# An AdaLN-FFN kernel on one core: the two low-rank sessions of each step made one, with the down products and the outputs moved behind it

## The reference

```python
# block 0: gated FFN with a low-rank adapter for each sequence, then a layer with a binarised weight
gate = x @ W_gate.T + 0.5 * (x @ A_gate[i].T) @ B_gate[i].T      # 512 -> 1376, rank 16
up   = x @ W_up.T   + 0.5 * (x @ A_up[i].T)   @ B_up[i].T
act  = silu(gate) * up
down = act @ W_down.T + 0.5 * (act @ A_down[i].T) @ B_down[i].T  # 1376 -> 512
x1 = x + down @ sign(weight).T + bias0
# block 1: rank-16 adapter for each sequence, then a layer with 8 summed adapters
z  = (x1 @ B1[k].T) @ A1[k].T
out = x1 + z @ W1.T + bias1 + 2 * sum_n w_n * (z @ lora_A[n].T) @ lora_B[n].T
```

## Time and profile before

| | us |
|---|---|
| median of 3 runs (862.29 to 863.07) | 863.04 |
| the profiled execution | 861.99 |
| its span | 860.2 |
| PE busy | 851.8 |
| DVE busy | 636.8 |
| ACT busy | 290.1 |
| POOL busy | 83.4 |

### The profile page before, as it was taken

The page is one execution under the profiler, slowest core; times in us unless marked ns, Lnnn a source line. Parts: engine busy times, 40 slices in busy tenths (PEclk is TensorE's granted clock), DMA queues, the critical chain, the costliest instruction groups (busy, mean ns, idle before and its releaser), DMA issues.

```text
span 860.2 us, 22295 instructions
## 1 busy us (share of the span) xinstructions
PE 851.8 (99%) x7384; PEld 695.8 (81%) x7384; DVE 636.8 (74%) x1362; ACT 290.1 (34%) x535; POOL 83.4 (10%) x122
## 2 busy tenths in 40 slices
PE   8999999999999999999999999999999999999998
PEld 5887788878888888888888888888888788888885
DVE  5697787868777786867778686777878686777764
ACT  4862333323233332323233332333333232323310
POOL 0202100101010010101001010100001010100101
PEclk9999999999999999999999999999999999999999
DMA  9969987869789796979889796978979797987953
GB/s 341 415 246 339 322 266 230 275 214 303 249 282 279 247 280 211 279 241 311 253 255 294 217 278 220 312 242 291 269 243 261 227 298 238 294 268 243 288 142 109
DMA packets 171356, 227.31 MB, mean 264 GB/s; under 512 B 59200, under 2 KB 128832, under 8 KB 163648
## 3 DMA queue, kind: packets, MB, share of 16 engines
q1 hardware_dynamic: 108480, 106.57, 42.2%
q10 hardware_dynamic: 60416, 111.27, 37.6%
q0 software_dynamic: 2432, 9.11, 2.7%
HBM read 178.69 MB, written 16.97 MB: 227 GB/s over the span
## 4 chain that ended last, share of the span: by engine, by line
PE 94%; DMA 2%; DVE 2%; ACTq 0%; POOL 0%; ACT 0%; issue 0%; SPq 0%; DVEq 0%
PE gu_ps L1246 52%; PE y_ps L1367 27%; PE gu_ps L1476 3%; PE out_ps L1389 3%; PE out_ps L1440 2%; PE y_ps L1246 1%; PE gu_ps L1467 1%; PE out_ps L1376 1%; PE out_ps L1246 1%; DMA t_table<-t_lo 1%; DMA x_in<-in_x 1%; PE out_ps L1397 1%; DVE vt_raw L987 0%; PE gu_ps L1367 0%; DMA lb_raw<-in_lbw 0%; POOL vt_table L602 0%
## 5 line engine op out<-in xcount | busy, mean ns | idle before, releaser
L1367 PE MATMUL y_ps<-down_sb,actT_sb 128*128 128x512 f32 x1023 | 248.1, 395 | 0.0
L1367 PEld LDWEIGHTS y_ps<-down_sb,actT_sb 128*128 128x128 f32 x1023 | 189.6, 188 | 59.6 <-issue 21.4
L626 ACT CAST actT_sb<-landed 128x512 fp32r<-128x512 f32 (+1 forms) x96 | 51.5, 582 | 130.7 <-issue 107.2
L578 POOL TENSOR_TENSOR b_two<-b_raw,const_sb 128x128 f32<-128x128 f32 x62 | 26.7, 451 | 656.7 <-DMA b_raw<-in_b1tab 656.7
L1246 PE MATMUL gu_ps<-wg_sb,xT_sb 128*128 128x432 f32 x384 | 82.3, 363 | 0.5 <-DVE act_all L915 0.5
L1246 PE MATMUL gu_ps<-wu_sb,xT_sb 128*128 128x432 f32 x384 | 81.7, 361 | 0.0
L1246 PEld LDWEIGHTS gu_ps<-wg_sb,xT_sb 128*128 128x128 f32 x384 | 71.0, 188 | 5.7 <-DVE xT_sb L897 1.4
L1246 PEld LDWEIGHTS gu_ps<-wu_sb,xT_sb 128*128 128x128 f32 x384 | 70.9, 188 | 4.2
L897 DVE TENSOR_TENSOR vslot<-vslot_raw,vslot 128x864 fp32r<-128x864 f32 x61 | 62.5, 1065 | 11.3 <-ACT vslot L626 11.2
L1246 PE MATMUL gu_ps<-slot,s_sb 128*128 128x512 f32 x270 | 69.0, 390 | 0.0
L919 DVE STREAM_TRANSPOSE act_all<-act_all 128x512 f32<-128x512 f32 (+1 forms) x96 | 64.1, 667 | 3.3
(11 more groups left out here) (188 smaller groups left out, 1263.7 us busy)
## 6 DMA issues: line engine op xcount, KB each, us to landing
slot<-t_table ACTq DMA_DIRECT2D x59, 1024.0 KB, 8.7
vslot_raw<-vt_table ACTq DMA_DIRECT2D x60, 432.0 KB, 4.1
a_raw<-in_atab SPq DMA_DIRECT2D x128, 152.0 KB, 7.6
rows_sb<-in_btab SPq DMA_DIRECT2D x128, 118.0 KB
landed<-act_all SPq DMA_DIRECT2D x190, 64.0 KB, 4.2
x_in<-in_x SPq DMA_DIRECT2D x31, 256.0 KB, 2.7
out_x<-out_sb SPq DMA_DIRECT2D x31, 256.0 KB, 5.2
xT_raw<-in_xT ACTq DMA_DIRECT2D x30, 256.0 KB, 3.3
```

The source lines that it names most:

```text
L578: nc.gpsimd.tensor_tensor(b1_two[:, n].rearrange("p k e r -> p e k r"), rows, ones, ALU.mult).then_inc(L["b1_moved"], 1)
L626: return nc.scalar.copy(o, i)
L1367: last = nc.tensor.matmul(to[:], actT_sb[:, ACTT_SLOT[c] + n, a, :], down_sb[:, blk, b, :], start=begin and (c, n) == (0, 0) and (a, b) == ...
```

## The change

One session a step. The small products now stand directly ahead of the row products, and are those of the **next** step for t (g + 1), of the step before for td (g - 1) and of three steps before for t1 (g - 3). They go into spare columns (from 432 on) of the SIDE and FIRST banks of `gu_ps`, which DVE sets to zero ahead of them (`clear`, three a step; PE waits for `cleared` before it writes these banks). The row products use td of g - 2 and t1 of g - 4. All 33 down products of g - 2 run at the start of step g, and y is complete when the row products have added their part. Each engine's step is split into `step` (ahead of the session) and `behind` (after it); DVE's `turn_t` for the next step, `split_xT`, `own_t1`, `own_td`, `turn_x1` and `add_out` stand in `behind`. x1 is made in place of x in `x_in`; POOL adds the bias from there into `x1_two[parity]`, a pair of buffers, where `add_out` adds in place and from where SP stores. The transposed x1 has places of its own over buffers that are idle then. The A-down rows have a buffer (`ad_raw`) and DMAs of their own, issued by ACT; loads of xT, slots and side blocks are issued earlier in ACT's step. The first six steps are written out instead of four. `finish` of each engine works off the longer pipeline: SP issues the sbd, and three sets of c rows, for the end (`c_end`) there.

The diff, cut to its core (removed functions are in the listing above):

```diff
...
-        x1_turn = x_in
+        x1_two = [place(f"x1_{n}", [P, H], f32) for n in range(2)]
...
+        t_at, td_at, t1_at = (gu_ps[5], SIDE), (gu_ps[3], SIDE), (gu_ps[2], SIDE)
...
+        def load_ad(engine, at):
+            for b in range(GB):
+                engine.dma_start(ad_raw[:, b, :], atab[bass.ds(at[b], P), AW:AW + ADW]).then_inc(L["ad_in"], 16)
...
+            def store(g, parity, signal=L["stored"]):
...
+                sp.dma_start(out[bass.ds(g * P, P), :], x1_two[parity][:]).then_inc(signal, 16)
+
+            def behind(g, parity):
+                if some(g + 2):
+                    turned_cond = table_rows(SP, 0, g + 2)
+                if some(g - 1):
+                    down_cond = table_rows(SP, 0, g - 1)
+                    next_post = table_rows(SP, 1, g - 1)
+                if some(g - 3):
+                    out_post = table_rows(SP, 1, g - 3)
+                next_cond = table_rows(SP, 0, g + 1)
+                if some(g + 2):
+                    sp.wait_ge(L["small_mm"], g + 2)
+                    load_a(turned_cond)
+                if some(g - 1):
+                    sp.wait_ge(L["first_mm"], g + 1)
+                    load_sbd(sp, down_cond)
+                if some(g - 3):
+                    load_c(sp, out_post)
+                if parity == 1 or first(g):
+                    send_act(sp, g, 1)
+                if not first(g):
+                    send_act(sp, g, 2)
+                sp.wait_ge(L["second_mm"], g + 1)
+                load_b(next_cond)
+                if some(g - 2):
+                    send_x1(sp, g - 2, parity, range(2, 4))
+                if some(g - 4):
+                    store(g - 4, parity)
+                if some(g - 1):
+                    if isinstance(g, int) and g == 1:
...
+                    after(sp, L["x1_turned"], g - 1)
+                    after(sp, L["x1_biased"], g - 1)
+                    load_x(g - 1)
+                    load_b1(g - 1, next_post)
...
-            def add_bias1(g):
-                pool.wait_ge(L["x1_turned"], g + 1)
-                nc.gpsimd.tensor_tensor(x1_sb[:], x1_sb[:], bias_sb[:], ALU.add).then_inc(L["x1_biased"], 1)
+            def add_bias1(g, parity):
+                pool.wait_ge(L["x1_done"], g + 1)
+                if some(g - 2):
+                    pool.wait_ge(L["stored"], 16 * (g - 1))
+                of = x_end[g] if isinstance(g, int) and g in x_end else x_in
+                nc.gpsimd.tensor_tensor(x1_two[parity][:], of[:], bias_sb[:], ALU.add).then_inc(L["x1_biased"], 1)
...
+            def next_ad(g):
+                at = table_rows(ON_ACT, 0, g)
+                act.wait_ge(L["ad_moved"], PAIRS * g)
+                load_ad(act, at)
...
+            def clear(of, w):
+                bank, at = of
+                nc.vector.memset(bank[:, at:at + w], 0.0).then_inc(L["cleared"], 1)
...
+                of = x_end[g] if isinstance(g, int) and g in x_end else x_in
+                if of is x_in:
+                    dve.wait_ge(L["x_in"], 16 * g + 16)
+                else:
+                    dve.wait_ge(E["x_in"], 2 * 16)
+                dve.wait_ge(L["first_mm"], g + 3)
+                nc.vector.tensor_tensor(of[:], of[:], y_ps[:], ALU.add).then_inc(L["x1_done"], 1)
...
+            def add_out(g, parity, bank=out_ps):
+                dve.wait_ge(L["first_mm"], min(g + 5, G + 2) if isinstance(g, int) else g + 5)
                 dve.wait_ge(L["x1_biased"], g + 1)
...
+                nc.vector.tensor_tensor(x1_two[parity][:], x1_two[parity][:], bank[:], ALU.add).then_inc(L["out_done"], 1)
...
+            def behind(g, j, parity):
+                if some(g - 2):
+                    add_y(g - 2)
                 for c in range(NC):
                     gated(g, c)
                     turn_act(g, c)
...
+                if some(g + 1):
+                    split_xT(g + 1, 1 - parity)
+                if last(g):
+                    return
+                if parity == 1 and not seven(j):
+                    first_sums(j + 1)
                     low_s(1, j + 1)
                     low_s(2, j + 1)
+                dve.wait_ge(L["second_mm"], g + 1)
+                if some(g - 3):
+                    own_t1(L["t1_ready"], t1_at)
+                if some(g - 1):
+                    own_td(g - 1, td_at)
+                if some(g - 3):
+                    dve.wait_ge(L["t1_ready"], g - 2)
+                clear(t1_at, TWO)
+                clear(td_at, TWO)
+                if some(g - 2):
+                    turn_x1(g - 2, parity)
+                if some(g - 4):
+                    add_out(g - 4, parity)
+                if parity == 1:
+                    low_side_t(1, j + 1)
+                    low_side_t(2, j + 1)
+                turn_t(g + 1, t_at)
+                clear(t_at, T_W)
                 if first(g):
                     dve.wait_ge(S["vraw_in"], 4 * 16)
...
+            def read_and_cleared(g, name):
+                pe.wait_ge(L["cleared"], 3 * g + 1 + ("t1", "td", "t").index(name))
...
+            def small(g, j, parity):
+                if some(g + 1):
+                    pe.wait_ge(L["a_in"], 16 * GB * (g + 2))
+                    pe.wait_ge(xT_in(1 - parity), 16 * (j + parity) + 16)
+                read_and_cleared(g, "t")
+                if some(g - 1):
+                    td_rows_ready(g - 1)
+                if some(g - 3):
+                    t1_rows_ready(g - 3)
+                if some(g + 1):
+                    last = t_rows(1 - parity, t_at)
+                if some(g - 1):
+                    last = low_rank_rows(some(g - 3), td_at, t1_at)
                 last.then_inc(L["small_mm"], 1)
 
             def out_rows(n, r=2, rows=rows_sb, to=out_ps, at=slice(0, H)):
                 return nc.tensor.matmul(to[pair(n), at], lhs_sb[group(r), pair(n)], rows[group(r), n, at],
...
+            def lora_ready(g):
                 pe.wait_ge(L["lhs2_in"], g + 1)
                 pe.wait_ge(L["b_in"], 2 * 16 * GB * (g + 1))
...
+                if some(g - 2):
+                    pe.wait_ge(L["td_ready"], g - 1)
+                    pe.wait_ge(L["sbd_in"], 16 * GB * (g - 1))
+                if some(g - 4):
+                    pe.wait_ge(L["t1_ready"], g - 3)
+                    pe.wait_ge(L["c_in"], 16 * GB * (g - 3))
+                    after(pe, L["out_done"], g - 4)
...
+            def step(g, j, parity):
+                if some(g - 2):
+                    after(pe, L["x1_done"], g - 2)
+                    for c in range(NC):
...
+                if seven(j):
+                    summed("vgate_odd" if parity else "vup_even", j)
+                small(g, j, parity)
+                lora_ready(g)
+                first_rows(g)
                 second_rows()
...
```

More of the change, by code:

```diff
@@ L408, in store_half @@
             engine.wait_ge(L["out_done"], g + 1 + half)
-            engine.dma_start(out[g * P:(g + 1) * P, columns(half)], x1_turn[:, columns(half)]).then_inc(L["stored"], 16)
+            engine.dma_start(out[g * P:(g + 1) * P, columns(half)], x_in[:, columns(half)]).then_inc(E["stored"], 16)
         def rows_stored(engine):
@@ L708, in step @@
                     copy_q1(j)
-                    send_x1(act, pp, range(0, 2))
+                if some(prev):
+                    next_ad(g)
+                if first(g):
+                    high_t(1)
+                    high_t(2)
+                copy_lhs(g)
+                if parity == 1 and some(g + 2):
+                    next_xT(g)
+                    load_xT(act, g + 2, parity)
+                if parity == 0 and seven(j):
                     high_s(4, j)
@@ L1055, in step @@
                         odd_products(g, j, prev)
-                elif prev is not None:
+                elif some(prev):
                     for c in range(NC):
@@ L1063, in step @@
                     low_t(1)
-                turn_t(g)
-                if pp is not None:
-                    own_t1(L["t1_ready"])
-                if prev is not None:
-                    own_td(g)
-                if first(g):
+                    turn_t(0, (out_ps, 0))
                     dve.wait_ge(S["t_raw"], t_count(4))
@@ L1074, in step, with behind @@
                     low_side_t(4, j)
-                if parity == 1 and nxt is not None:
+                if parity == 1 and some(g + 1) and seven(j):
                     first_sums(j + 1)
-                if nxt is not None:
-                    split_xT(nxt, 1 - parity)
-                if pp is not None:
-                    after(dve, L["stored"], 16 * pp)
-                    add_out(pp)
+                    low_s(1, j + 1)
+                    low_s(2, j + 1)
+            def behind(g, j, parity):
+                if some(g - 2):
+                    add_y(g - 2)
                 for c in range(NC):
@@ L1500, in step @@
                     first_gate(g)
-                    small_ready(g, prev, pp)
-                    small(parity, prev, pp)
```

(10 more changed lines are left out.)

526 lines of the change are left out of this document (270 added, 256 removed).

## The result

The changed kernel takes **1181.05 us** (median of 4 runs, 1174.81 to 1182.04), the kernel before 863.06 beside it (862.29 to 864.32): a ratio of **1.366**, 95% interval 1.364 to 1.368. The forecast was 1038, with a range to 1115. The direction was right, the size was not.

What follows compares the result with a forecast made beforehand. PE bound the kernel before; after it, SP's 47.95 us plus two 7.55 us waits, less 1.2, made 61.9 us a pair. 26 periods of 30.95 us, with start and tail, gave 1038 us; range 950 to 1115.

Steps and rivals of the forecast that it cites:

- SP as second bound: SP's queue of DMA issues: 46.15 us of own work in a 49.36 us pair before, 47.95 after the change.
- The step that decides: a wait behind its own store: In SP's behind(g), x load waits for POOL's bias addition, which waits for the store's landing: 7.55 us a step.
- L: Time from SP's issue of the result store to its landing: taken as 6.6 us, rows from 2.0 to 10.3.
- The sessions: Joining PE's two tiled sessions saves one entry and exit a step: net 0.1 to 0.15 us, 4 us in all.
- add_y's race on y_ps: DVE's add_y must read y_ps before the next down products overwrite it: PE stands 0.3 us a step.
- rival A: The forecast itself, chance 0.84: PE waits some 6 us a step for x1_done, hiding PE's small losses and gains.
- DVE's order: DVE operations added between gating and first sums of an odd step cost PE some 0.8 us a pair.
- B: SP's wait is shorter than read; only PE's new races count, 1.15 us a pair: 879 us, chance 0.06.
- C: SP's issues get faster, own work falls to 43.5 us, PE decides again: 855 us, chance 0.05.
- D: PE, idle 6 us a step, stays at its lower clock within the step: over 1300 us, chance 0.03.
- E: Gains and losses cancel: 862 to 864 us, chance 0.02.
- A's own signs: One PE idle stretch a step ahead of down products, PE share near 80%, SP waits 5 to 10 us a step.

Runs made afterwards that it cites:

- b1: Kernel before, with SP waiting for its store's landing right behind the store and nothing else changed: 972.5 us.
- e5: Changed kernel with GpSimd issuing the stores and ScalarE all four sends of the transposed x1; whole computation: 882.8 us.
- e10: Changed kernel with row products ahead of small products, stores and x load on GpSimd, sends on ScalarE, SP's sbd and c loads before its small-products wait: 892.3 us.
- r4: Kernel with both loops removed (r3), the load of x moved ahead of the eight B loads: 1024.1 us.
- e7: Changed kernel with only SP's order changed: store behind c loads, then sends, four B loads, x load, four B loads, b1 load: 1089.8 us.
- e4: Changed kernel with GpSimd's queue issuing the stores as soon as DVE's addition is done; whole computation: 1051.5 us.
- e9: Changed kernel with only all four sends of the transposed x1 moved to ScalarE's queue; whole computation: 1070.2 us.
- r3: Changed kernel with both loops cut: stores and sends take a constant tile's data, waits for their landings removed or replaced: 973.6 us.
- r6: Changed kernel with ScalarE's T-table loads moving half of each 1 MB, same loads, waits and places: 1136.8 us.

## Why the prediction was right or wrong

**What bounds the kernel, and SP as second bound: right.** SP's own work in a pair was forecast at 47.95 us, 46.75 with the 1.2 taken off for less crowded queues, and measured at 46.4; 27 waits of SP for POOL's bias addition, as counted.

**The step that failed: "The step that decides: a wait behind its own store", with "I take the mean, 6.6" for the landing L.** The wait was there as read, twice a pair; its term was too small, and the sum had no term at all for a second loop beside it.
- The size of L: 4.3 us a pair. SP stood 19.4 us a pair behind its stores, against 2 x 7.55 = 15.1 forecast. The store lands 8.8 us after its issue at the median. I had seen that the odd place has the slot loads beside it with 8.9 and that the new order brings them there in both parities, and still took the mean with the 4.3 of a place that no longer exists. The 2.6 us that the prediction takes from the Trainium skill (DMA: Bandwidth & Descriptors, Anatomy of one DMA) are by a formula that the page gives for DMAs issued from GpSimd; the stores on SP's queue land earlier than that with no table near (2.0, b1) and far later behind the tables.
- The missing loop: 5.9 us a pair. The forecast took the new places of the buffers as storage and did not ask who writes there. The changed kernel has it in two lines that the excerpt of the diff leaves out, `x1_turn` over `s0_sb` and over `u4_sb`, with a wait of DVE ahead of u4 and of the first sums. Some 2 of the 5.9 us are PE's lower clock behind the wait (last section).

Together 10.2, less 0.35 for SP's own work: 9.85 us, which is the 71.7 us read for the 61.9 forecast. By the table above this is 122 of the 143 us missed: steps 4 to 31 take 290.9 us more than before, where the forecast's sum has 1035.5 - 860.2 - 6.1 = 169.2. Another 14.5 are the start, priced at nothing, where the same second loop makes its first turn, and 7 the tail, 13.2 us longer where 6.1 were forecast.

**The sessions: right in sign, and small as said.** Net 0.1 to 0.15 us a step was forecast, 0.12 came out, though for another order of the streams; in the forecast's own order the same starts give 284 + 183 + 465 + 213 = 1145 ns, 0.09 us less than before, if nothing waits. The runs show a gap at the join in both directions, 183 and 464 ns. The Trainium skill (TensorEngine Tiling (Array Packing), Tiling Modes, Key Properties, and not the section that the prediction names) has a change of mode drain PE; by that the saving is at the low end, and the trace agrees.

**add_y's race on y_ps, 0.3 us: right.** In the changed kernel the exit behind the rows takes 727 ns (622.240 to 622.967) for 464, so 0.26; in e5 728 and 792. In the changed kernel it costs nothing, as rival A says, for PE waits longer elsewhere.

**DVE's order, 0.8 us a pair: not in the form forecast.** In e5, where it would show, an odd step takes 21.13 us for 20.90, and the race on y_ps is enough for that; the 0.8 us showed in e10 alone, with the Silus held 1.3 us.

**Rivals.** B's price, 879 us, is near that of e5, 882.8, by luck: B had 1.15 us a pair, e5 has 0.7 (50.10 for 49.38) and 8.4 us more in the tail, for which B has no term. C had SP's issues give way to 43.5 us; they hold SP for 46.4. D was right that the clock falls and wrong that it would not come back: behind the long idle stretch the windows read 0.50, then 0.57, then 1.00 (last section). E is out. A's own signs held in part: PE's share is 78%, but PE has two kinds of idle stretch, and the longer is not the one named.

## What to carry to other kernels

A landing time here goes with the moment of issue and not with the transfer: before a row of before is carried over, look at what the other queues issued in the 7 us ahead of the new place, and take the row that had that neighbour. A queue that is within 7% of being the bound, as SP's was, has no room to wait for its own transfers. Moving one waited-for transfer out of a burst can hand the delay to the next in the queue, as r4 and e7 did; giving it to another queue helped in all of e4, e9 and e5. And where a diff lays a buffer over another, write down both sets of readers and the wait between them before anything else is priced.

## What the runs showed of the hardware

The same 64 KB of one tile land 2.2 us after issue ahead of a burst of tables and 8.9 us inside it, issued 11 us apart by two queues; the same 256 KB load takes 2.7 us at the median in the changed kernel and 9.9 in r3. A store of 256 KB from SP's queue landed in 2.0 to 3.2 us with no table issued in the 9 us ahead of it (the loop of b1), and in 7.3 to 10.3 with four of them 4 to 7 us ahead (b1 and the kernel before). How much of this is the tables' bytes stays open: with a third of the burst taken away (r6) it fell by 1.3 us only. Stores of 256 KB from GpSimd's queue, issued as soon as the sum was there, landed in 3.0 to 3.6 us at the median.

PE's clock behind an idle stretch, sums by window of the changed kernel (columns as above):

```profile
597.50:607.50 10.00, 1.68 (x9) 1.21 (x7) 0.00 (x0) 0.00 (x0) 0.00 (x0) 0.83 0.94 349
607.50:610.00 2.50, 0.00 (x0) 0.00 (x0) 2.01 (x3) 0.00 (x0) 1.26 (x1) 0.50 0.02 9
610.00:615.00 5.00, 5.00 (x14) 4.29 (x15) 4.19 (x9) 3.17 (x5) 0.00 (x0) 0.57 0.45 131
615.00:620.00 5.00, 5.00 (x76) 4.54 (x79) 2.38 (x3) 0.40 (x1) 0.00 (x0) 1.00 0.00 0
```

PE had nothing to do from 599.2 to 610.0. The granted clock read 0.50 at its end, the lower of the two levels, and the first six products of 512 columns took 2.93 us where the same number took 1.54 at 596.47:

```profile
596.47 1.54 PE L1349 MATMUL gu_ps<-w_sb,xT_sb 128*128 128x512 f32 x6
```

```profile
610.00 2.93 PE L1349 MATMUL gu_ps<-w_sb,s_sb 128*128 128x512 f32 x6 [10.82 <-DVE s_sb L960]
```

The six products of 432 columns behind them took 2.08 us for 1.34. So an idle stretch of 10.8 us costs some 2 us more on the chain behind it, which is on top of what the wait itself takes and stands in the small products' lateness.

The change between the two tiled streams is not symmetric: 32-column tiles to 32-row tiles 183 ns where PE does not wait (e5), 32-row to 32-column 464 ns (e10), start to start.
